# Loading the adjacency stream of a four-layer graph network in pairs of units, with x and u issued between the first pairs

## What is computed

```python
h = jnp.maximum(_layernorm(x, axis=-1), 0.0)
x = x + _L0_gnn_ref(h, adj, L0_gnn_u)        # adj @ (h * (u >= 0.1) / 0.9)
h = jnp.maximum(_layernorm(x, axis=-1), 0.0)
x = x + _L1_gnn_ref(h, adj, L1_gnn_W, L1_gnn_b)   # (adj @ h + h) / degree, a linear layer, relu, L2 norm
h = jnp.maximum(_layernorm(x, axis=-1), 0.0)
x = x + _L2_gnn_ref(h, adj, L2_gnn_W)        # D^-1/2 (adj + I) D^-1/2 @ h, a linear layer
h = jnp.maximum(_layernorm(x, axis=-1), 0.0)
x = x + _L3_gnn_ref(h, adj, L3_gnn_W)        # adj @ h / (degree + 1), a linear layer
```

## Time and profile before

| | us |
|---|---|
| median of 3 runs (lowest, highest) | 1948.39 (1947.73, 1948.98) |
| the profiled execution's own time | 1948.27 |
| its span, first to last instruction | 1946.5 |
| TensorE matmuls busy | 1911.3 |
| VectorE busy | 854.7 |
| ScalarE busy | 115.2 |
| packets of the load queue, share of 16 DMA engines | 87.0% |

### The profile page before, as it was taken

One profiled execution on the slowest core, in us unless ns is written; L12 is line 12 of the kernel. 1 busy time (PEld: TensorE's weight loads), 2 busy tenths in 40 slices (PEclk: granted clock), 3 DMA queues, 4 the chain that ended last, 5 costly groups with the idle time before them and its releaser, 6 DMA issues.

```text
span 1946.5 us, 21454 instructions
## 1 busy us (share of the span) xinstructions
PE 1911.3 (98%) x9008; PEld 670.1 (34%) x9008; DVE 854.7 (44%) x1023; ACT 115.2 (6%) x293; POOL 11.3 (1%) x29
## 2 busy tenths in 40 slices
PE   6999999999999999999999999999999999999998
PEld 2333333333333333333333333333333333333343
DVE  8778999988877762622112111321211100110322
ACT  0000000000000001100000000111100000000000
POOL 0000000000000000000000000000000000000000
PEclk9999999999999999999999999999999999999999
DMA  9999999999888875497888887397999989999997
GB/s 387 421 421 422 420 421 421 421 418 355 337 329 313 304 293 193 199 362 283 294 291 290 293 299 281 157 404 287 385 378 369 352 302 422 372 366 415 351 422 330
DMA packets 93646, 670.53 MB, mean 344 GB/s; under 512 B 11120, under 2 KB 11120, under 8 KB 12656
## 3 DMA queue, kind: packets, MB, share of 16 engines
q1 hardware_dynamic: 92160, 666.94, 87.0%
q0 software_dynamic: 768, 2.10, 0.3%
q10 hardware_dynamic: 624, 0.13, 0.0%
HBM read 667.03 MB, written 2.10 MB: 344 GB/s over the span
## 4 chain that ended last, share of the span: by engine, by line
PE 93%; DVE 5%; DMA 2%; issue 0%; ACT 0%; POOL 0%; SPq 0%; DVEq 0%
PE acc L507 87%; PE Z L549 3%; DMA ring<-stream_in 1%; PE DEG L559 1%; DVE row_sum L933 1%; PE DEG L567 1%; PE HT L590 1%; DVE inverse L837 0%; DVE mean L833 0%; DVE row_sum L836 0%; DVE h L852 0%; DVE row_sum L834 0%; DMA h<-u_in 0%; DVE h L854 0%; DVE h L876 0%
## 5 line engine op out<-in xcount | busy, mean ns | idle before, releaser
L507 PE MATMUL acc<-ring,h 128*64 128x512 f32 x7744 | 1697.1, 594 | 28.0 <-DMA ring<-stream_in 19.4
L507 PEld LDWEIGHTS acc<-ring,h 128*64 128x64 f32 x7744 | 552.5, 137 | 1099.1 <-issue 1087.6
L933 DVE TENSOR_TENSOR row_sum<-row_sum,ring 128x2048 f32<-128x2048 f32 x187 | 428.5, 2292 | 9.0 <-DMA ring<-stream_in 3.7
L868 DVE TENSOR_TENSOR z_sb<-Z,deg_rsqrt 128x256 f32<-128x256 f32 x16 | 6.8, 424 | 345.0 <-PE Z L549 344.9
L900 DVE TENSOR_TENSOR y<-acc,y 64x512 f32<-64x512 f32 x16 | 11.0, 684 | 284.0 <-PE acc L507 276.6
L507 PE MATMUL acc<-diag,h 128*64 128x512 f32 x448 | 103.0, 592 | 0.0
L372 ACT COPY y<-acc 64x512 f32<-64x512 f32 x45 | 26.1, 581 | 992.5 <-PE acc L507 714.3
L549 PEld LDWEIGHTS Z<-below,y 128*128 128x128 f32 x512 | 61.9, 191 | 54.3 <-issue 27.6
L994 DVE TENSOR_TENSOR y<-acc,y 64x512 f32<-64x512 f32 x36 | 24.6, 683 | 112.5 <-PE acc L507 112.2
L549 PE MATMUL Z<-below,y 128*128 128x64 f32 x512 | 70.7, 281 | 2.2 <-DVE y L995 2.2
L507 PEld LDWEIGHTS acc<-diag,h 128*64 128x64 f32 x448 | 32.6, 137 | 64.8 <-issue 64.1
(11 more groups left out here) (75 smaller groups left out, 354.6 us busy)
## 6 DMA issues: line engine op xcount, KB each, us to landing
ring<-stream_in SPq DMA_DIRECT2D x604, 1024.0 KB, 9.2
diag<-stream_in SPq DMA_DIRECT2D x28, 1024.0 KB, 11.1
x<-x_in SPq DMA_DIRECT2D x4, 512.0 KB, 6.7
h<-u_in SPq DMA_DIRECT2D x4, 512.0 KB, 7.6
x_out<-x POOLq DMA_DIRECT2D x16, 128.0 KB, 5.8
below<-w_in ACTq DMA_DIRECT2D x6, 16.0 KB, 5.7
bias<-b_in ACTq DMA_DIRECT2D x1, 32.0 KB, 7.7
```

The source lines that it names most:

```text
L507: return nc.tensor.matmul(half_of(bank, half), h[layer % 2][:, J * F:(J + 1) * F], moving, start=start, stop=stop)
L933: nc.vector.tensor_tensor(row_sum[:, :], before, slot(key)[:, :], ALU.add).then_inc(unit_summed, 1 if count > 1 else 2)
```

## The change

Two units of one row b whose g differ in the last bit alone (14 and 15, 12 and 13, ...) and that follow each other in the list of loads are now one transfer of 2 MB. In DRAM two such units are interleaved, so that each partition has one run of 16 KB; a unit that is loaded by itself takes 8 KB runs that lie 16 KB apart. The ring is one tensor of 12 slots; a pair takes two neighbouring slots, in the order of g, and is not formed across the ring's end. It is issued when both older units in those slots are let go, and it has one semaphore, on which the users of either unit wait. A diagonal unit is never part of a pair, and ends one that might have been formed across it. Of 604 units in the ring 476 are in 238 pairs, and 128 are loaded by themselves; there are 394 transfers of adj instead of 632. The eight loads of x and u are issued a quarter at a time, one quarter ahead of each of the first four pairs. The instructions of the other engines stay as they were.

The core of the diff:

```diff
+def transfers_in_order():
+
+    out, n = [], 0
+    for key in LOADS:
+        if key[0] == "diag":
+            out.append([key])
+            continue
+        before = out[-1][0] if out and len(out[-1]) == 1 else ("diag",)
+        if before[0] == key[0] and before[1] == key[1] and before[2] ^ 1 == key[2] and (n - 1) % RING != RING - 1:
+            out[-1] = sorted([before, key])
+        else:
+            out.append([key])
+        n += 1
+    return out
+
+
+TRANSFERS = transfers_in_order()
+PLACED = [key for transfer in TRANSFERS for key in transfer if key[0] != "diag"]
+PLACE = {key: n for n, key in enumerate(PLACED)}
...
         def loaded(key):
-            return unit_loaded[PLACE[key] % RING], 16 * (PLACE[key] // RING + 1)
+            first, count = ARRIVALS[key]
+            return unit_loaded[first], 16 * count
...
-            for q in PROLOGUE:
-                part = slice(q * quarter, (q + 1) * quarter)
-                sp.dma_start(x[:, part], x_in[:, part]).then_inc(xu_loaded[q], 16)
-                sp.dma_start(u[:, part], u_in[:, part]).then_inc(xu_loaded[q], 16)
-            for key in LOADS:
...
+            for place, transfer in enumerate(TRANSFERS):
+                if place < QUARTERS:
+                    q = PROLOGUE[place]
+                    part = slice(q * quarter, (q + 1) * quarter)
+                    sp.dma_start(x[:, part], x_in[:, part]).then_inc(xu_loaded[q], 16)
+                    sp.dma_start(u[:, part], u_in[:, part]).then_inc(xu_loaded[q], 16)
...
+                n = PLACE[transfer[0]]
+                for before in PLACED[max(n - RING, 0):max(n - RING + len(transfer), 0)]:
+                    sp.wait_ge(*freed(before))
+                    if before in SUMMED:
+                        sp.wait_ge(unit_summed, SUMMED[before] + 1)
+                at = n % RING * UNIT
+                sp.dma_start(ring[:, at:at + len(transfer) * UNIT], source).then_inc(unit_loaded[n % RING], 16)
...
     a = np.asarray(adj).reshape(P, ROWS, TPR, P, ROWS, TPR).transpose(1, 4, 3, 5, 2, 0)
+    a = a.reshape(ROWS, ROWS // 2, 2, P, UNIT).transpose(0, 1, 3, 2, 4)
```

More of the change, by code:

```diff
@@ L105, with arrivals @@
 RING_LOADS = [key for key in LOADS if key[0] != "diag"]
-PLACE = {key: n for n, key in enumerate(RING_LOADS)}
+USE = {key: n for n, key in enumerate(RING_LOADS)}
+def transfers_in_order():
[14 more added lines that the diff above has]
+PLACE = {key: n for n, key in enumerate(PLACED)}
+def arrivals():
+    out, told = {}, [0] * RING
+    for transfer in TRANSFERS:
+        if transfer[0][0] != "diag":
+            first = PLACE[transfer[0]] % RING
+            told[first] += 1
+            out |= {key: (first, told[first]) for key in transfer}
+    return out
+ARRIVALS = arrivals()
 DIAGS = {key: n for n, key in enumerate(key for key in LOADS if key[0] == "diag")}
@@ L113, in units_let_go @@
     for phase in (2, 3):
-        at = PLACE[(phase, *HEAD_PLACE[phase](FIRST_A[0][0]))]
+        at = USE[(phase, *HEAD_PLACE[phase](FIRST_A[0][0]))]
         ended = [(phase, *HEAD_PLACE[phase](job)) for step in SECOND_D for job in step]
@@ L149, in gnn_stack @@
         u = h[1]
-        ring = [sbuf(f"ring{i}", [P, UNIT]) for i in range(RING)]
+        ring = sbuf("ring", [P, RING * UNIT])
         diag = [sbuf(f"diag{i}", [P, UNIT]) for i in range(2)]
@@ L238, in slot @@
         def slot(key):
-            return ring[PLACE[key] % RING]
+            at = PLACE[key] % RING * UNIT
+            return ring[:, at:at + UNIT]
         def loaded(key):
-            return unit_loaded[PLACE[key] % RING], 16 * (PLACE[key] // RING + 1)
+            first, count = ARRIVALS[key]
+            return unit_loaded[first], 16 * count
         def diag_slot(phase, b):
@@ L290, in _ @@
             quarter = TILES * F // QUARTERS
-            for q in PROLOGUE:
-                part = slice(q * quarter, (q + 1) * quarter)
-                sp.dma_start(x[:, part], x_in[:, part]).then_inc(xu_loaded[q], 16)
-                sp.dma_start(u[:, part], u_in[:, part]).then_inc(xu_loaded[q], 16)
-            for key in LOADS:
-                if key[0] == "diag":
-                    n = DIAGS[key]
+            for place, transfer in enumerate(TRANSFERS):
[4 more added lines that the diff above has]
+                    sp.dma_start(u[:, part], u_in[:, part]).then_inc(xu_loaded[q], 16)
+                kind, b, g = transfer[0]
+                if kind == "diag":
+                    b = g
+                source = stream_in[b, g // 2][:, g % 2 * UNIT:(g % 2 + len(transfer)) * UNIT]
+                if kind == "diag":
+                    n = DIAGS[transfer[0]]
                     if n >= 2:
                         sp.wait_ge(diag_freed, n - 1)
[L300 to L309, removed]
+                    sp.dma_start(diag[n % 2][:, :], source).then_inc(diag_loaded[n % 2], 16)
+                    continue
+                n = PLACE[transfer[0]]
[5 more added lines that the diff above has]
+                sp.dma_start(ring[:, at:at + len(transfer) * UNIT], source).then_inc(unit_loaded[n % RING], 16)
         @block.gpsimd
@@ L1081 @@
         "u_in": np.asarray(L0_gnn_u).reshape(P, TILES * F),
-        "stream_in": a.reshape(ROWS, ROWS, P, UNIT),
+        "stream_in": a.reshape(ROWS, ROWS // 2, P, 2 * UNIT),
         "w1_in": np.asarray(L1_gnn_W),
```

## The result

| | before | after |
|---|---|---|
| median of the runs on one chip, us | 1948.24 (8 runs, 1947.64 to 1948.98) | 1953.7 (8 runs, 1952.49 to 1956.54) |
| profiled execution: its own time / its span, us | 1948.27 / 1946.5 | 1952.49 / 1950.7 |
| ratio of the times, 95% interval | | 1.0028 (1.0019 to 1.0037) |

Slower by 0.28%, 5.5 us between the medians, and more than the 0.2% that can be told from no change. The profiled execution of after is the fastest of its eight and is 4.2 us over that of before. Its trace can account for these 4.2 us; the other 1.2 are beyond it. The slowest execution of after was 4 us over its fastest, that of before 1.3.

A forecast was written before the change was run, and what follows sets the result against it. TensorE's matmuls bound the kernel (1911.3 of 1946.5 us), with transfers keeping pace in two stretches only; 1.0 us lost at the start plus 1.2 at the end, on 1948.27, gave 1950.5, range 1948.0 to 1955.0.

The forecast's parts named there:

- the clock's: Rival: TensorE's clock falls in the new stall before unit 15 of row 1, costing 1.9 us, to 1952.4; chance 0.27.
- no saving: Rival: the 2 MB transfers go no faster than before, so the pace gain falls away, giving 1952.7; chance 0.10.
- the slower runs': Rival: the new 8 KB and 16 KB runs lose 3% of pace in a full queue, giving 1961.6; chance 0.10.
- The lead costed at nothing: Start: TensorE begins at 14.6 instead of 18.1, but the 3.5 us become a longer wait for VectorE's row total.
- VectorE's second quarter 0.4 late: Start: x and u data for VectorE's second quarter land 0 to 1.1 us late, taken as 0.4; total at 62.2.
- Pace 1.6% better: Full load queue: pairs save 1.6%, 0.04 us a unit, 0.6 us by unit 15 of row 1.
- Stall of 3.4 before unit 15, pair landing at 59.6: Start: TensorE stands still from 56.2 to 59.6 until pair (14, 15) of row 1 lands; 0.7 us lost.
- Row 1's total at 104.4: Start: VectorE's sum of row 1 comes 1.2 us later, at 104.4; the start loses 1.0 us in all.
- The middle at nothing: Between the two full-queue stretches: 238 fewer issues, and the later ones, cost nothing, with over 10 us left.
- (a): End: behind (4, 14, 15) the queue idles and row 13's pair lands 0.5 to 2.1 us behind, taken as 1.3.
- (b): End: the saving of 1.6% over 113 us moves the last landing by -1.8 us (0 to -3.4).
- (c): End: TensorE has two units of the last row to do behind the last byte instead of one, +1.74 us.

## Why the forecast came out as it did

The range held the time (1953.7 in 1948.0 to 1955.0). Its likeliest case, 1950.5 and within 0.2%, was wrong by 3.2 us of the median and 2.0 of the profiled execution. No case that the prediction worked out gives 1953.7: the clock's gives 1952.4, no saving 1952.7, and the slower runs' 1961.6, which did not occur. The range held by its width, which is luck in part.

- **The lead costed at nothing**: right. It began at 14.76 (forecast 14.6), and the runs with x and u first and between single units show it worth nothing.
- **VectorE's second quarter 0.4 late**: 0.13 in the profiled execution (14.62 against 14.49), but 1.36 in that of the kernel with matmuls in the stall (15.85), which has the same loads. The place varies by about a us between executions, which I had from one trace.
- **Pace 1.6% better**: 1.2%. The 0.4% are 0.2 us at the start and 0.5 at the end.
- **Stall of 3.4 before unit 15, pair landing at 59.6**: 2.78 us and 60.0, with 0.97 + 1.24 us of waits on the way where the sum had 1.5. Right, and so is total 0 at 62.5 but for 0.4, had the clock stayed.
- **The failed step is the sum's assumption that it stays.** The rival "the clock falls in the new stall", given 0.27, took place. It cost 1.4 us there, priced 1.9, and an estimated 0.65 by T, since VectorE binds next. My price took no account of that.
- **Row 1's total at 104.4**: 105.16. The addition that waits for unit 9 came 2.15 us later (75.94 against the earlier trace rows), where I had 1.4. The pair was there only 0.3 us ahead of the later of its two units before, whose addition began at 76.25. The sum took 2.49 - 1.4 = 1.1 for that: 0.7 for 18 units' saving, and 0.4 for "what the queue gained", which no run shows. This row alone puts the start at 1.85 of its 2.51 us, over my upper end of 1.6.
- **The middle at nothing**: right, no wait for a transfer from 110 to 1900 us. The 2.0 us a transfer, 476 us of queue time by the prediction, are given by the Trainium skill, DMA: Bandwidth & Descriptors, in its section on the anatomy of one DMA, for transfers that GpSimd issues. In this queue of SyncE's the pace rose by 1.2% and the middle took as long as before.
- **The end, (a) and (b), last landing earlier by 0.5**: 1914.0 + 26.3 = 1940.3 is 2.5 later, just T's delay, so (a) and (b) together are 0.0. What each is by itself, forecast 1.3 and -1.8, single executions don't tell.
- **(c) +1.74**: right, by after's rows. The last landing is as far from T as before, and TensorE's work behind it is 1.71 us longer. What the sum did not see is that pair (12, 13) ends at the same time, so that splitting the last pair alone gives back 0.34, and both 1.37.
- **Waits for transfers of 1.3 us in all before**: too few. Two more, 0.77 us at 1920.21 and 0.90 at 1930.55, which the profile calls "issue", end just as a unit lands (1897.0 + 23.1 = 1920.1, and 1905.1 + 25.4 = 1930.5). TensorE had caught up with the stream three rows before the end. The sum doesn't use this number.

Summed: 1.0 became 2.5, 1.2 became 1.7, and 2.2 became 4.2. What stays open is the rest of the 5.5 us between the medians. The varying start and the clock's fall in some executions and not in others are seen in traces, but how often each occurs in the runs was not measured. For the same reason the split of T's 2.51 us into clock and VectorE is an account of one trace; the times of the two kernels made to keep the clock up, 1952.79 and 1952.32, are too close to 1953.7, and of another chip, to settle it.

## What to carry to other kernels

When two transfers become one, the first half arrives as late as the second. Go through the places where the consumer has caught up with the stream, here the start and the end, and price there the first unit of each pair by what the consumer could do with it; leave the transfers apart at those places and join them elsewhere. Where undoing one join gives nothing back, look for a second limit at the same place before clearing the first. A head start is worth what the next join lets through: look up what else must be there (here a vector engine's sum, and 0.2 us behind it the stream itself) before counting it. A faster full queue is worth nothing where the queue was not waited for.

## What the runs showed of the hardware

- The same gap of 2.78 us in TensorE's work let the clock fall in two of three traced executions and not in the third. A stall of this length is to be priced with a chance, not with yes or no.
- 16 KB runs go at 426 GB/s and 8 KB runs at 421 in a full queue, and 8 KB runs 16 KB apart at 421 as well. The pairs gave 1.2%; whether by the longer run or by fewer transfers, no run tells apart.
- The first landings vary: the load that VectorE's second quarter needs let it begin at 14.62 us in one execution and at 15.85 in another, of two kernels with the same loads. In the second, pair (14, 15) of row 1 landed at about 61.9 instead of 60.0.
